# Softmax row sums of a pair of heads in one group of products over four column groups of 32, with the divisions and the projections some slots later

## What is computed

```
q       = einsum('bld,dhk->blhk', x, Wq)
latent  = einsum('bld,dc->blc', x, Wkv_down)
k, v    = einsum('blc,chk->blhk', latent, Wk_up), einsum('blc,chk->blhk', latent, Wv_up)
attn    = softmax(where(causal, einsum('bqhd,bkhd->bhqk', q, k) / sqrt(64), min))
y       = einsum('bqhd,hdo->bqo', einsum('bhqk,bkhd->bqhd', attn, v), Wout)
x1      = layernorm(x + y)
out     = layernorm(x1 + experts(x1))     # top-1 of 32, capacity 1.25 T / E
```

## Time and profile before

| | |
|---|---|
| three runs, median | 2701.8 us (2698.88 to 2704.28) |
| profiled execution, its own time | 2698.37 us |
| its span | 2696.5 us |
| mean granted TensorE clock | 0.969 of full |
| busy: TensorE, VectorE, ScalarE, GpSimd | 2506.9, 1549.8, 1002.1, 1701.6 us |
| first addition of the first and of the last pair | 78.80 and 2281.93 us |

### The profile page before, as it was taken

How to read it: one execution, slowest core, us unless ns; L and a number is a source line. 1 busy time by engine, 2 the same in 40 slices (tenths; PEclk the granted TensorE clock), 3 DMA queues, 4 the chain that set the end, 5 groups by cost and what they waited for, 6 DMA issues and landing times.

```text
span 2696.5 us, 35905 instructions
## 1 busy us (share of the span) xinstructions
PE 2506.9 (93%) x12072; PEld 1594.3 (59%) x12072; DVE 1549.8 (57%) x4370; ACT 1002.1 (37%) x1496; POOL 1701.6 (63%) x1671
## 2 busy tenths in 40 slices
PE   7999999999999999999999999999999999769996
PEld 5555665556655665566556655565556655536664
DVE  3666556665666566655665566646665665135553
ACT  2344424442444334433443344424443344112222
POOL 0677656865687658766786568656866588214444
PEclk7999999999999999999999999999999999879998
DMA  8000000200020001100110002000200010044541
GB/s 233 21 20 17 17 9 17 67 17 13 17 63 17 13 13 44 40 13 17 40 40 17 13 17 64 17 13 17 63 17 16 13 40 24 16 147 150 161 152 59
DMA packets 97574, 118.91 MB, mean 44 GB/s; under 512 B 12992, under 2 KB 76488, under 8 KB 97392
## 3 DMA queue, kind: packets, MB, share of 16 engines
q1 hardware_dynamic: 90224, 99.98, 13.6%
q0 software_dynamic: 7168, 16.64, 1.7%
HBM read 46.91 MB, written 37.90 MB: 31 GB/s over the span
## 4 chain that ended last, share of the span: by engine, by line
PE 66%; POOL 17%; issue 9%; DVE 5%; ACT 2%; DMA 1%; SPq 0%; POOLq 0%; ACTq 0%; DVEq 0%
PE value_ps L675 14%; POOL sums L433 9%; PE turned_ps L652 8%; PE row_ps L628 7%; PE turned_ps L655 7%; PE misc_ps L576 6%; PE turned_ps L784 5%; PE misc_ps L693 5%; PE misc_ps L685 4%; POOL probs L409 2%; PE value_ps L797 2%; PE misc_ps L797 2%; POOL slots_x L464 2%; ACT probs L862 1%; DVE masked_row L1010 1%
## 5 line engine op out<-in xcount | busy, mean ns | idle before, releaser
L862 ACT ACTIVATE probs<-turned_ps 128x1024 f32<-128x1024 f32 (+3 forms) x768 | 616.5, 811 | 941.2 <-PE turned_ps L655 919.0
L433 POOL TENSOR_TENSOR sums<-sums,probs 128x1024 f32<-128x1024 f32 (+3 forms) x512 | 830.3, 1622 | 22.9 <-ACT probs L862 13.9
L1010 DVE CUSTOM_DVE_ANT_0 masked_row<-row_ps,future 128x128 bf16<-128x128 f32 (+3 forms) x1024 | 464.2, 488 | 410.2 <-PE row_ps L628 409.2
L675 PE MATMUL value_ps<-probs,lat_keys 128*64 128x512 f32 (+3 forms) x3072 | 606.9, 507 | 48.1 <-POOL probs L409 43.7
L652 PE MATMUL turned_ps<-q_hl,lat_hi 128*128 128x512 f32 (+3 forms) x1536 | 568.5, 378 | 0.0
L655 PE MATMUL turned_ps<-q_max,lat_lo 65*128 65x512 f32 (+3 forms) x1536 | 528.0, 352 | 2.4 <-DMA q_max<-max_rows 2.4
L409 POOL TENSOR_SCALAR_AFFINE_SELECT probs<-probs 128x256 f32<-128x256 f32 x512 | 209.9, 410 | 482.8 <-ACT probs L862 481.9
L628 PE MATMUL row_ps<-lat_hi,q_hl 128*128 128x512 f32 (+3 forms) x1536 | 453.1, 367 | 12.0 <-DVE unit_max L1010 7.1
L652 PEld LDWEIGHTS turned_ps<-q_hl,lat_hi 128*128 128x128 f32 x1536 | 293.4, 191 | 197.0 <-issue 148.5
L429 POOL TENSOR_TENSOR sums<-probs 128x768 f32<-128x768 f32 (+1 forms) x128 | 268.6, 2099 | 218.8 <-ACT probs L862 218.8
L675 PEld LDWEIGHTS value_ps<-probs,lat_keys 128*64 128x64 f32 x3072 | 180.2, 137 | 352.5 <-issue 219.7
(11 more groups left out here) (165 smaller groups left out, 2344.9 us busy)
## 6 DMA issues: line engine op xcount, KB each, us to landing
q_max<-q_hl SPq DMA_DIRECT2D x256, 128.0 KB
slots_x<-headsT SPq DMA_DIRECT2D x40, 258.0 KB, 8.9
ex_x<-slots_x SPq DMA_DIRECT2D x64, 129.0 KB, 3.4
x_in<-in_L_attn_x_bld SPq DMA_DIRECT2D x8, 1024.0 KB, 6.2
layer_out<-x_in SPq DMA_DIRECT2D x8, 1024.0 KB, 4.8
ex_w<-in_L_ffn_w_gate SPq DMA_DIRECT2D x32, 256.0 KB, 2.8
ex_w<-in_L_ffn_w_up SPq DMA_DIRECT2D x32, 256.0 KB, 3.1
ex_w<-in_L_ffn_w_down SPq DMA_DIRECT2D x32, 256.0 KB, 3.6
```

Of the source, the lines that this page charges most:

```text
L433: nc.gpsimd.tensor_tensor(sums[c][:, :, q0:BANK], sums[c][:, :, q0:BANK], now[:, :, q0:BANK], ALU.add).then_inc(added, 1)
L675: mm = nc.tensor.matmul(value_ps[h * LD:(h + 1) * LD, q0:BANK], lat_keys[b % 2][:, j, :], probs[:, n % NPROBS, h, q0:BANK], start=(j == 0) ...
L862: nc.scalar.activation(probs[:, n % NPROBS, :, q0:BANK], turned_ps[n % 2][:, :, q0:BANK], ACT.Exp).then_inc(exp_done, 1)
L1010: nc.vector.tensor_tensor_reduce(masked_row[n % 2][:, 0:width], row_ps[n % 2][:, 0:width], future[:, BANK - width:], scale=-1.0, scalar=-M ...
```

## The change

One use of the bank for a pair's row sums instead of two. `total` multiplies both halves' sums of both heads by a matrix of ones with 32 columns; the four results stand in four column groups of 32 (partitions 0 to 31: head 0, half 0; then head 0, half 1; head 1, half 0; head 1, half 1). It comes in slot 2 of the next pair. The division's reciprocals are taken twice, and four copies of 32 partitions bring each half's reciprocals also to the other group of its head. The divisions move to GpSimd's slots 5 and 7; GpSimd's first copy into `sums[0]` waits for the one product, the first addition of half 1 no longer waits for a product of its own. Projection tiles go to slots 7, 9, 10, 11 of pair 0 and 3, 5, 7, 9 of pair 1, the second variance from slot 8 to slot 10 of pair 1.

```diff
-        rinv = sb("rinv", [P, BANK // 32], F32, attn)
+        rinv = sb("rinv", [P, 2, BANK // 32], F32, attn)
...
             if gp:
-                late[4].append(("sums", gp - 1, 1))
-            late[6].append(("sums", gp, 0))
+                late[2].append(("sums", gp - 1))
...
             if b and p == 0:
-                for i, t in enumerate((3, 5, 7, 10, 11)):
+                for i, t in enumerate((7, 9, 10, 11)):
                     late[t].append(("proj", b - 1, i))
             if b and p == 1:
-                for i, t in enumerate((3, 5, 7)):
-                    late[t].append(("proj", b - 1, 5 + i))
+                for i, t in enumerate((3, 5, 7, 9)):
+                    late[t].append(("proj", b - 1, HPB + i))
...
-        ENDING = ([("sums", PAIRS - 1, 1)] + [("proj", LAST, i) for i in range(NT)]
+        ENDING = ([last_sums] + [("proj", LAST, i) for i in range(NT)]
...
                     if gp:
-                        pool.wait_ge(misc_full, MISC["sums", gp - 1, 0] + 1)
+                        pool.wait_ge(misc_full, MISC["sums", gp - 1] + 1)
                     nc.gpsimd.tensor_copy(sums[0][:, :, 0:P], now[:, :, 0:P]).then_inc(added, 1)
                 elif j == 1:
-                    if c == 1 and gp:
-                        pool.wait_ge(misc_full, MISC["sums", gp - 1, 1] + 1)
...
-                    if gp and t == 0:
-                        divide(gp - 1, 0)
-                    if gp and t == 6:
-                        divide(gp - 1, 1)
+                    if gp and t in (5, 7):
+                        divide(gp - 1, t // 7)
...
-            def total(gp, c):
-                use = ("sums", gp, c)
+            def total(gp):
+                use = ("sums", gp)
                 bank = take(use)
-                pe.wait_ge(added, gp * NADD + (HPB if c == 0 else NADD))
+                pe.wait_ge(added, (gp + 1) * NADD)
                 for h in range(2):
-                    mm = nc.tensor.matmul(bank[h * LD:(h + 1) * LD, :], ones_f[:, :], sums[c][:, h, :], start=True, stop=True)
+                    for c in range(2):
+                        k = 2 * h + c
+                        mm = nc.tensor.matmul(bank[k * 32:(k + 1) * 32, :], ones_f[:, 0:32], sums[c][:, h, :],
+                                              start=True, stop=True)
                 mm.then_inc(full_of(use), 1)
...
-            def invert_rows(gp, c):
-
-                use = ("sums", gp, c)
-                n = 2 * gp + c
-                wait_emptied(dve, use)
-                nc.vector.reciprocal(rinv[:, :], sums_cols[:, :].rearrange("p (n q) -> p n q", q=32)[:, :, 0]
-                                     ).then_inc(inverse_done, 1)
-                dve.wait_ge(inverse_done, n + 1)
-                if gp:
-                    dve.wait_ge(normalised, n - 1)
-                nc.vector.transpose(rinv_rows[c][:, :], rinv[:, :].unsqueeze(2).to_broadcast([P, BANK // 32, 32])
-                                    ).then_inc(inverse_rows, 1)
+            def invert_rows(gp):
+                wait_emptied(dve, ("sums", gp))
+                cols = sums_cols[:, :].rearrange("p (n q) -> p n q", q=32)[:, :, 0]
+                for c in range(2):
+                    nc.vector.reciprocal(rinv[:, c, :], cols).then_inc(inverse_done, 1)
+                dve.wait_ge(inverse_done, 6 * gp + 2)
+                for c in range(2):
+                    for h in range(2):
+                        src, dst = (64 * h + 32 * k for k in (c, 1 - c))
+                        nc.vector.tensor_copy(rinv[dst:dst + 32, c, :], rinv[src:src + 32, c, :]).then_inc(inverse_done, 1)
+                for c in range(2):
+                    dve.wait_ge(inverse_done, 6 * gp + 4 + 2 * c)
+                    if gp:
+                        dve.wait_ge(normalised, 2 * gp + c - 1)
+                    nc.vector.transpose(rinv_rows[c][:, :], rinv[:, c, :].unsqueeze(2).to_broadcast([P, BANK // 32, 32])
+                                        ).then_inc(inverse_rows, 1)
...
-                    if b and (p, t) in ((0, 11), (1, 8)):
+                    if b and (p, t) in ((0, 11), (1, 10)):
                         variance(b - 1, p)
```

More of the change, by code:

```diff
@@ L230, in build_layer @@
         EARLY, LATE = {}, {}
+        last_sums = ("sums", PAIRS - 1)
         for gp in range(PAIRS):
@@ L1025, in copy_max, with invert @@
                 nc.vector.tensor_copy(max_rows[c][:, :], bank[0:NT, 0:P]).then_inc(misc_free, 1)
-            def invert(gp, c):
-                use = ("sums", gp, c)
+            def invert(gp):
+                use = ("sums", gp)
                 bank = wait_full(dve, use)
                 nc.vector.transpose(sums_cols[:, :], bank).then_inc(free_of(use), 1)
-            def invert_rows(gp, c):
-                use = ("sums", gp, c)
-                n = 2 * gp + c
-                wait_emptied(dve, use)
-                nc.vector.reciprocal(rinv[:, :], sums_cols[:, :].rearrange("p (n q) -> p n q", q=32)[:, :, 0]
-                                     ).then_inc(inverse_done, 1)
-                dve.wait_ge(inverse_done, n + 1)
-                if gp:
-                    dve.wait_ge(normalised, n - 1)
-                nc.vector.transpose(rinv_rows[c][:, :], rinv[:, :].unsqueeze(2).to_broadcast([P, BANK // 32, 32])
-                                    ).then_inc(inverse_rows, 1)
+            def invert_rows(gp):
[14 more added lines that the diff above has]
+                                        ).then_inc(inverse_rows, 1)
             def statistics(b, i):
```

## The result

The changed kernel takes 3016.8 us (median of 4 runs, 3012.68 to 3018.78) against 2700.34 for the kernel before, measured beside it: ratio 1.117, interval 1.1155 to 1.1186. The forecast was 2787 in a range of 2730 to 2845. The direction was right; the loss is 316 us where 87 was worked out.

What follows compares the result with a forecast made beforehand. The prediction took the kernel as a TensorE queue with detours, 66% of the chain. Per-pair terms over all pairs summed to +86.9 us, giving 2785 against the profiled 2698.4, stated as 2787; range 2730 to 2845.

Steps and rivals of the forecast that it cites:

- VectorE's queue: Whole inversion in slot 3 takes 2.47 us ahead of slot 4's maxima, delaying slot 6 by 1.40 us in a pair without extra work.
- slot 9: Pair 0 and 1 projections in slot 9 wait for VectorE to empty q from the shared bank: +2.5 us each.
- The product: Row-sum product in slot 2: four column groups together take 1.01 us, replacing two products of 0.96: -0.91 us a pair.
- the rival of two at a time: Four column groups don't run together; the row-sum product costs 1.9 us, +0.9 in 62 pairs: 2842 us; chance 0.15.
- The bank: Slot 2's row-sum product waits until VectorE empties q from the shared bank: +0.80 us, with slot 3 queued behind.
- The copies: Four 32x16 VectorE copies in the inversion, 0.18 us each without overlap: 0.72 us; bounds 0.28 to 0.8.
- the plain pair: Pair without extra work: 0.80 - 0.91 + 1.40 = +1.29 us, 13 such pairs, +16.8 us.
- The clock: TensorE's clock could drop after 2.5 us waits: up to 14 spells of 1.7 us, +24 us, outside the sum.
- Pairs 4 and 5: GpSimd's sends delay the mask, TensorE waits near 1.8 us, replacing shorter mask waits: +0.2 us a pair, x14 = +2.8.
- Pairs 1 and 2: Division leaves GpSimd's queue ahead of the mask, returning 1.28 us; with other terms +0.56 and +0.2 us a pair.
- Rival 2: VectorE's slot 3 inversion is hidden because TensorE runs behind or it is short; only bank waits count: 2715 us, chance 0.10.
- Rival 3: VectorE empties q before TensorE finishes slot 2's values, so neither bank nor inversion stops TensorE: 2624 us, chance 0.08.

## Why the prediction was right and wrong

- **Direction: right**, and from the right places. Bank, VectorE's queue, slot 9, the layer norm, routing and the next x all show in the list of waits.
- **The product: right.** 0.99 us for eight matmuls, four column groups together; the rival of two at a time is out. The 1.25 that I worked out from the Trainium skill (TensorE: Matmul & The Clock Gate, Part 3: Packing small matmuls) is too high for this case. The same section's model adds about 4 ns for each further tile; the trace is near it, with starts 7 ns apart within the four of a pass.
- **The bank: right.** 0.73 us in pair 3 where I had 0.80; 61 waits of 0.61 on average.
- **The copies: the first step that failed.** I took "the nearest small operation", a conversion of 128x8 to integers at 0.16 us, and put the upper end of the four copies at 0.8 us. They measured 2.04 in pair 3 and 4 x 0.582 = 2.33 on average. The nearest row was near in size, but at all eight of its runs GpSimd was idle, so it could not show the wait that VectorE's copies have beside GpSimd; whether such a conversion has it too, no run shows. The queue was thus 3.69 us (181.64 to 185.33) instead of 2.47, and slot 3 to slot 6 took 7.56 instead of 6.50. With reciprocals of 0.245 us the plain pair came to 30.9, against the 30.8 of my working. The Trainium skill (SBUF — State Buffer, SBUF: two separate sides) states such a rule: VectorE and GpSimd share a pair of ports under an exclusive lock, held for a whole instruction, which VectorE needs in its two-port modes, and an fp32 copy within SBUF uses these. The trace agrees: slowed copies end some 0.03 us after GpSimd's instruction. The reciprocals don't wait.
- **The copies held one by one: right.** Each starts 0.03 us after the one before has ended, as the rule of the Trainium skill has it (VectorE: DVE Perf Modes, Two Vector instructions with no wait between them).
- **The clock: the second step that failed, and the larger one.** I gave +24 us at the most, for the 14 long waits alone, and the sum has nothing for it. It cost some 160 to 180. Waits of under 2 us, several in a pair, brought it on as well. Where it stayed full, the working came out: with reciprocals pairs 0 and 1 of batches 1 to 7 together last 4.3 us longer than before, where I had 4.4 (a projection tile of pair 0 now falls into pair 1). Pairs 4 and 5, at a clock of 0.90, last 3.6 longer where I had 0.2.
- **How the loss divides.** Changed against before: 316 us. Reciprocals give back 129, with about 143 us less at half clock (0.935 of 2884.1 us: 375). TensorE's idle time fell by 54 of them and its busy time by 74, so by this estimate the copies' own waits are near 55 and the clock that fell behind them near 75; at 0.45 a microsecond it would be 65 and 64. Of the other 187, the clock has some 90 to 105 (208 us more at half clock than before), and the waits and the saved product, forecast at 87, have the rest, 80 to 95.
- **Pairs 1 and 2**: the division's 1.28 us did come back (the waits there fell from 1.6 to 0.3 and from 2.1 to 0.3 us), but the changed kernel's waits for masks are 37.4 us in all, against 43.7 before. In pairs 4 and 5 the sends took what was won, as the working said (near 1.8 us a pair; it measured 2.0), but I put the pair at +0.2 because this wait should cover VectorE's queue. These pairs last 37.3 us, where 31.0 was the time before: the wait covered the queue only in part (0.65 us of it is left in pair 4 of batch 1), and with the clock at 0.86 some 10 us of the pair run at half, worth near 4.7.
- **Small slips of the working**: pair 2 is 7 x 0.21 = 1.5, not 1.3, and the maxima of pair 3's slot 4 end near 9.52, not 9.45. Neither matters.
- **Rival 2 (the queue hidden)** is out: TensorE's row products waited 52.8 us for it.
- **Rival 3 (faster)** did not come true in this kernel. Of the kernels run here, one with the product was faster than the one before only when q left the bank first, the inversion stood in two other places and the sends were out of GpSimd's way, and then it took 2654.7 us, not the 2624 of the rival.

## What to carry to other kernels

Price a small operation by its kind and its neighbours, not by its size: a 512-number copy on VectorE takes 0.17 us or up to 2.4, by what GpSimd does at that moment, and a reciprocal makes the same move without that wait. A row that is to stand for its price has to come from a moment when the other engine is busy. When a change puts two pieces of work into one, follow the queue it lands in: the product here saved 0.9 us of TensorE's time a pair and lost several in the order of VectorE's and GpSimd's work. On a kernel that TensorE bounds, count a wait at more than its length; here the clock that fell after the waits cost nearly as much again (some 160 to 180 us beside 201 of waits).

## What the runs showed of the hardware that was not expected

- Copies in fp32 within SBUF on VectorE can last until a GpSimd instruction ends: 0.161 to 2.395 us for the same 32x16, and all 113 of over 0.30 us end 0.02 to 0.04 after one. It isn't so beside every instruction: 14 copies that ran beside a send took 0.161 to 0.164. Reciprocals of the same shape in the same place: 0.241 to 0.251 us.
- Work without use made the kernel faster: 270 matmuls more, 49 us less, with the mean granted clock at 0.941 instead of 0.914. The half clock followed waits of 0.3 to 1.6 us, several of them in pair 3 of batch 0; 3.4 us of it cost pair 7 of batch 5 1.6 us.
- Four column groups of 32 work as well together as two of 64: 1.06 us for eight matmuls, 1.08 for four.
